# The last work of two routed layers: 32 pairs of tiles and 7 single tiles in place of 39 pairs

## The chip, the cores and the metric

The kernel runs on one core of a Trainium2 chip. A core has five engines with their own instruction streams, which meet only at semaphores: TensorE (PE, matrix products into PSUM), VectorE (DVE), ScalarE (ACT), GpSimd (POOL) and SyncE (SP, which here issues DMAs only). The metric is the device time of one launch in microseconds (us), lower is better. All times below are of one core, and the profile is of one execution.

## The reference, cut to what matters

Input x has 4096 tokens of 128 numbers. The program is a mixture-of-experts layer, an attention-like layer, and the same mixture-of-experts layer again, each added to x:

```python
x = x + 0.5 * ffn(layernorm(x))
x = x + attn(layernorm(x))
x = x + 0.5 * ffn(layernorm(x))

def ffn(h):                                   # D=128, F=512, E=8 experts, K=2 of them per token
    probs = softmax(h @ gate_W.T)
    top_v, top_i = top_k(probs, 2)
    routed = sum over the 2 chosen experts e of
             top_v * ((silu(h @ w1_e[e]) * (h @ w3_e[e])) @ w2_e[e])
    shared = (the same form with 8 small experts, for every token) / 8
    return 0.5 * shared + 0.5 * routed
```

Two choices per token make 8192 (token, expert) rows. They are sorted by expert, and each expert's rows are filled up to whole tiles. All is float32.

## The kernel before, in words

**Two layers.** The loop `for l in range(2)` on every engine does the mixture layer twice; the attention lies between. A layer is: normalise and score the tokens; the shared experts' first chunks ("front", `FRONT` = 7 of 8 chunks of 512 tokens in layer 0, 6 in layer 1) on PE, while DVE and ACT work out the routing; the routed tiles; the remaining shared chunks, while the results come back from DRAM.

**Routing on DVE.** `slots_of` counts each expert's rows, rounds them up, and gives every row a place (`cum`, `pos`). Its steps are a chain: each is followed by a wait for its own semaphore (`route.then`). `batch` turns places into two small one-hot factors that ACT scales (`pairs`) and PE multiplies into `psT`, in 16 batches. `table` makes from it the row numbers (`source`, `target`), and `experts` the weight offset of each pair of tiles (`w_off`). In layer 0 eight `low_part` steps of 128x1024 come after it on DVE.

**Routed tiles.** A tile is 128 rows of one expert; the kernel does `PT` = 2 tiles of one expert as a pair, since both use one set of weights. 8192 rows of 8 experts need at most `PAIRS` = 39 pairs, so `RUN` = 78 tiles a layer, whatever the routing is. POOL fetches a tile's rows with one indirect DMA (`fetch_row`), for groups of `GT` = 4 tiles, three groups ahead; PE transposes them into `psT` (`transpose_rows`); DVE splits the transposed group into a high part `xTH` and a low part `xTL` (`copy_xT`); ACT copies the pair's weights into `w_high` and `w_low` (`weights_of`). Step by step PE then does, by the list of stages and delays of its `pipelined` call, `in_routed` of tile k-4, `look_up` (a register load for the pair's place in W2), `out_routed` of tile k-6, and `transpose_rows` of tile k:

```python
def product(out, a_high, a_low, b_high, b_low):
    pe.matmul(out, a_high, b_high, start=True, stop=False)
    pe.matmul(out, a_high, b_low, start=False, stop=False)
    return pe.matmul(out, a_low, b_high, start=False, stop=True)
```

`in_routed` makes four such products of 256 columns a step, which are half of the hidden features (two of four blocks) of both tiles of the pair: 12 matmuls in the type fp32r. `out_routed` makes 4 plain float32 matmuls of 128x128 a tile. Between them ACT makes `silu` of `psG`, and DVE `hT` = silu times `psU` (`gated_routed`). When a group's last tile is done, DVE scales the four outputs into `yout` (`copy_y`), and POOL scatters them to `results` in DRAM (`send_result`, one indirect DMA a tile, five groups behind the fetch). The last group is shorter (`LAST` = 2 tiles), and its tiles are scaled and sent one by one (`copy_y_last`), from two PSUM banks, `last_y`.

**End of a layer.** SP waits until every tile has been sent (`y_sent`), then loads `results` back: in layer 0 as `Y` in pieces for the attention, in layer 1 as `YF`, which is added into the output. Before that SP's last work in a layer is to write the tokens to DRAM. After its last `out_routed` PE does the remaining shared chunks.

The order of each engine's work is thus fixed by the program text. Lines named in the prediction: 1334 to 1336 (`product`), 1405 (`out_shared`), 1433 (`transpose_rows`), 1487 (`out_routed`), 830 to 854 (`slots_of`), 876 to 879 (`experts`), 908 (`low_part`), 980 (`copy_y`), 626 and 641 (fetch and send).

Of the kernel before, what the change touches and what calls it, by code (L numbers as in the profile page):

```python
# [13 lines left out]
P = 128  # L14
D = 128
NT = 4096
TILES = NT // P
E = 8
# [11 lines left out]
PAIRS = TOPK * NT // PAIR + E - 1  # L30
RUN = PT * PAIRS
TILES_R = RUN
# [130 lines left out]
def macaron(nc, x, w_qkvT, w_swigluT, w_outT, gateT, w1_e, w3_e, w2_e, w1_s, w3_s, w2_s, out):  # L163
    ctx = ExitStack()
    with ctx:
# [14 lines left out]
        def overlaid(*groups):  # L180
# [34 lines left out]
        pair_no = sb("pair_no", [P, PAIRS])  # L215
# [16 lines left out]
        pair_bits = sb("pair_bits", [P, 2, E], i32)  # L232
        npair = sb("npair", [P, E])
        tend = sb("tend", [P, E])
        tstart = sb("tstart", [P, E])
        base = sb("base", [P, E])
        pair_e = sb("pair_e", [P, PAIRS])
        w_off = sb("w_off", [P, PAIRS], i32)
# [24 lines left out]
            [("xTH", [P, 2, GT, P], fp32r), ("xTL", [P, 2, GT, P], fp32r)],  # L263
            [(name, [P, TILES, E], fp32) for name in ("logit", "prob", "cand", "onehot0", "onehot1", "pick")] +
            [(name, [P, E, TILES], fp32) for name in ("chosen", "cum")] +
            [("pair_cmp", [P, PAIRS, E], fp32)])
        xTH = memory["xTH"]
        xTL = memory["xTL"]
        logit = memory["logit"]
# [6 lines left out]
        pair_cmp = memory["pair_cmp"]  # L276
# [12 lines left out]
            [("Y", [P, 4, TOPK, TB, D], fp32), ("XNT", [P, NT], fp32)],  # L289
            [("hs", [P, 2, FT, CH * P], fp32),  # L290
# [7 lines left out]
        XNT = memory["XNT"]  # L298
        hs = memory["hs"]
# [61 lines left out]
        pair_weights = sem("pair_weights")  # L361
        consts = sem("consts")
# [88 lines left out]
        last_y = [psY, psT]  # L451

        block = ctx.enter_context(nc.Block())
        CONSTS = 13
# [6 lines left out]

        first_routed = [l * (SHARED + RUN) + front[l] for l in range(2)]

# [33 lines left out]
        def _(sp):  # L497
# [10 lines left out]
            for l in range(2):  # L508
# [6 lines left out]
                pipelined(sp, [(keep_tokens, 0)], CHUNKS, 2)  # L515

# [31 lines left out]
        def _(pool):  # L548
# [25 lines left out]
            pool.iota(pair_no[:, :], pattern=[[1, PAIRS]], base=0, channel_multiplier=0,  # L574
# [133 lines left out]
        def _(dve):  # L708
# [34 lines left out]
            for l in range(2):  # L743
                def gated(hidden, s, turn):

                    dve.wait_ge(silu_done, turn + 1)
                    dve.wait_ge(u_full, turn + 1)
                    dve.tensor_tensor(hidden, silu[:, s.u % 2, :], psU[:, s.u % 2, :], ALU.mult).then_inc(h_done, 1)  # L748
# [77 lines left out]
                def slots_of():  # L826
# [3 lines left out]
                    route.then(dve.tensor_scalar(pair_bits[:, 0, :], psY[:, E:2 * E], float(PAIR - 1), None, ALU.add))  # L830
                    route.then(dve.tensor_scalar(pair_bits[:, 1, :], pair_bits[:, 0, :], PAIR.bit_length() - 1, None,
                                                 ALU.logical_shift_right))
                    route.then(dve.tensor_copy(npair[:, :], pair_bits[:, 1, :]))
                    route.then(dve.tensor_tensor_scan(tend[:, :], ones[:, 0:E], npair[:, :], 0.0,
                                                      ALU.mult, ALU.add))
                    route.then(dve.tensor_tensor(tstart[:, :], tend[:, :], npair[:, :], ALU.subtract))
                    dve.scalar_tensor_tensor(base[:, :], tstart[:, :], float(PAIR), psY[:, 0:E], ALU.mult, ALU.add)\
                       .then_inc(ranks_read, 1)
# [5 lines left out]
                                                      ALU.mult, ALU.add))  # L844
                    shared_steps(1)
# [27 lines left out]
                def experts():  # L873

                    cmp3 = [P, PAIRS, E]
                    route.then(dve.tensor_tensor(pair_cmp[:, :, :], wide(pair_no[:, :], cmp3),
                                                 tend[:, :].unsqueeze(1).to_broadcast(cmp3), ALU.is_ge))
                    route.then(dve.tensor_reduce(pair_e[:, :], pair_cmp[:, :, :], X_AXIS, ALU.add))
                    dve.tensor_scalar(w_off[:, :], pair_e[:, :], float(E - 1), float(F),
                                      ALU.min, ALU.mult).then_inc(w_off_done, 1)  # L880
# [32 lines left out]
                def copy_xT(s):  # L913
# [14 lines left out]
                    dve.wait_ge(xT_link, g + (GROUPS * l + 1))  # L928
# [19 lines left out]
                def gated_routed(s):  # L948
# [5 lines left out]
                    dve.tensor_tensor(hT[:, s.u // PT % 2, half, :].rearrange("p f c -> p (f c)"), silu[:, s.u % 2, :],  # L954
                                      psU[:, s.u % 2, :], ALU.mult).then_inc(h_done, 1)
# [5 lines left out]
                def copy_y_last(par, t):  # L961
# [4 lines left out]
                    return dve.tensor_scalar(yout[:, par, t, :], last_y[t % 2][:, t * D:(t + 1) * D],  # L966
# [19 lines left out]
                if l == 1:  # L986
# [17 lines left out]
                    def add_sums(n):  # L1004
# [3 lines left out]
                        dve.tensor_tensor(xs, xs, last_y[n % 2][:, :], ALU.add).then_inc(last_added_sums, 1)  # L1008
# [119 lines left out]
        def _(act):  # L1128
            act.wait_ge(consts, CONSTS)
            for l in range(2):  # L1130
# [20 lines left out]
                def silu_of(s, turn):  # L1151
# [3 lines left out]
                    act.activation(silu[:, s.u % 2, :], psG[:, s.u % 2, :], ACT.Silu).then_inc(silu_done, 1)  # L1155

                def silu_shared(k):
                    silu_of(Step.of(k, 2), shared_at(l, k))
# [79 lines left out]
                for k in range(RUN):  # L1238
                    silu_of(Step.of(k, 2), first_routed[l] + k)
# [88 lines left out]
        def _(pe):  # L1328
# [11 lines left out]
            def table_entry(l, s):  # L1340


                key = (l, s.i // PT)
# [320 lines left out]
```

## Time and profile before

| | |
|---|---|
| runs | 731.95 us median of 3 (730.91 to 735.62) |
| profiled execution | span 733.5 us, from the first to the last instruction; the page gives no other time of this execution |
| PE | busy 660.3 us (90%) |
| DVE, ACT, POOL | busy 458.8, 411.3 and 430.6 us (63, 56 and 59%) |
| routed stage of layer 0, layer 1 | 112 to 299 us, 512 to 699 us |
| DMA | 45.91 MB, mean 63 GB/s |

How to read it: an engine's share is over the whole span, though the stages have different limits; so the stretches have to be read one by one. A stage is found in the 40 slices of the page, and its limit in the chain of waits, which is followed back from the last instruction. Matmuls of PE overlap, so the length of one says less than the distance from one start to the next. The plain float32 matmul of 128x128 shows as two records.

### The profile page before, as it was taken

Reading aid. Unit: us, or ns where it says so; the run is one execution under the profiler, and the core shown is the slowest. Engines: PE = TensorE matmul, PEld = TensorE weight load, DVE = VectorE, ACT = ScalarE, POOL = GpSimd, SP = SyncE. Lnnn points to the kernel's source line nnn. Section 1 sums busy time; section 2 is a strip of 40 time slices with the busy share of each in tenths; the row PEclk is TensorE's granted clock in tenths of the full one; section 3 lists DMA queues with packets and bytes.
Section 4 is the critical chain, followed back from the end, with each engine's and each line's share of the span. In section 5 each row is a group of like instructions: output and inputs, shape, how many; then the busy total and the mean of one; then the engine's idle time right before and its main releaser. Section 6 shows DMA issues by size and latency. Waiting matters only on the chain.

```text
span 733.5 us, 14294 instructions
## 1 busy us (share of the span) xinstructions
PE 660.3 (90%) x4860; PEld 602.1 (82%) x4860; DVE 458.8 (63%) x1177; ACT 411.3 (56%) x861; POOL 430.6 (59%) x511
## 2 busy tenths in 40 slices
PE   3878999999999999957987777999999999999995
PEld 3767879999999999825654574888999999999983
DVE  6678895554445555359999867884555555544536
ACT  2658617666666666236654436664666666666520
POOL 5600075777777776489987424007577777777530
PEclk9989999999999999989999997999999999999999
DMA  9542011221222231131100002402212212212137
GB/s 296 231 78 40 1 42 38 56 52 52 52 55 52 52 53 44 57 105 44 47 12 1 0 1 46 73 2 49 40 55 54 52 52 56 51 53 52 43 104 261
DMA packets 35685, 45.91 MB, mean 63 GB/s; under 512 B 6432, under 2 KB 27936, under 8 KB 35232
## 3 DMA queue, kind: packets, MB, share of 16 engines
q1 hardware_dynamic: 25632, 24.39, 11.8%
q0 software_dynamic: 9984, 20.63, 11.5%
q8 instruction: 40, 0.66, 0.4%
q14 instruction: 29, 0.24, 0.1%
HBM read 28.41 MB, written 16.58 MB: 61 GB/s over the span
## 4 chain that ended last, share of the span: by engine, by line
PE 65%; DVE 20%; issue 4%; ACT 4%; POOL 3%; DMA 2%; SPq 1%; ACTq 0%; POOLq 0%; DVEq 0%
PE psY L1487 18%; PE psG L1334 6%; PE psU L1336 6%; PE psG L1336 6%; PE psU L1335 6%; PE psG L1335 6%; PE psU L1334 6%; PE psH L1405 4%; DVE rec L1076 3%; PE psT L1433 2%; DVE hs L748 2%; DVE XN L738 2%; DVE ln_stats L725 1%; DVE xn L1060 1%; POOL results L641 1%
## 5 line engine op out<-in xcount | busy, mean ns | idle before, releaser
L626 POOL DMA_INDIRECT rows<-tokens,source x156 | 153.7, 985 | 156.3 <-DVE source L900 98.6
L1155 ACT ACTIVATE silu<-psG 128x512 f32<-128x512 f32 x220 | 131.1, 596 | 150.6 <-PE psG L1336 147.2
L954 DVE TENSOR_TENSOR hT<-silu,psU 128x512 f32<-128x512 f32 x156 | 107.4, 688 | 158.9 <-PE psU L1336 150.3
L641 POOL DMA_INDIRECT results<-yout,target x156 | 153.8, 986 | 63.3 <-issue 45.7
L1487 PE MATMUL psY<-W,hT 128*128 x1232 | 162.4, 275 | 1.8 <-DVE yout L980 1.8
L1487 PEld LDWEIGHTS psY<-W,hT 128*128 128x128 f32 x1232 | 150.4, 191 | 2.2 <-DVE hT L954 2.2
L1229 ACT ACTIVATE w_high<-W13H 128x1024 fp32r x78 | 82.7, 1061 | 59.0 <-PE psU L1336 54.8
L1334 PE MATMUL psG<-xTH,w_high 128*128 128x256 f32 x312 | 100.0, 321 | 0.7 <-ACT w_low L1229 0.7
L1336 PE MATMUL psG<-xTH,w_low 128*128 128x256 f32 x312 | 88.0, 282 | 0.0
L1336 PE MATMUL psU<-xTH,w_low 128*128 128x256 f32 x312 | 88.0, 282 | 0.0
L1335 PE MATMUL psU<-xTL,w_high 128*128 128x256 f32 x312 | 87.7, 281 | 0.0
L1335 PE MATMUL psG<-xTL,w_high 128*128 128x256 f32 x312 | 87.4, 280 | 0.0
L1334 PE MATMUL psU<-xTH,w_high 128*128 128x256 f32 x312 | 86.9, 278 | 0.0
L1229 ACT ACTIVATE w_low<-W13L 128x1024 fp32r x78 | 81.8, 1048 | 0.0
L748 DVE TENSOR_TENSOR hs<-silu,psU 128x512 f32<-128x512 f32 x64 | 43.7, 684 | 38.3 <-PE psU L1336 30.5
L1405 PEld LDWEIGHTS psH<-W2S,hs 128*128 128x128 f32 x512 | 59.4, 192 | 5.7 <-DVE hs L748 4.7
L1405 PE MATMUL psH<-W2S,hs 128*128 128x128 f32 x512 | 60.1, 276 | 2.9 <-DVE hs L748 2.9
L1334 PEld LDWEIGHTS psG<-xTH,w_high 128*128 128x128 f32 x312 | 59.2, 190 | 0.9 <-issue 0.9
L1335 PEld LDWEIGHTS psG<-xTL,w_high 128*128 128x128 f32 x312 | 59.3, 190 | 0.0
L1334 PEld LDWEIGHTS psU<-xTH,w_high 128*128 128x128 f32 x312 | 59.1, 190 | 0.0
L1336 PEld LDWEIGHTS psG<-xTH,w_low 128*128 128x128 f32 x312 | 58.8, 188 | 0.0
L1335 PEld LDWEIGHTS psU<-xTL,w_high 128*128 128x128 f32 x312 | 58.6, 188 | 0.0
(188 smaller groups left out, 1215.7 us busy)
## 6 DMA issues: line engine op xcount, KB each, us to landing
W<-w_e SPq DMA_DIRECT2D x3, 2048.0 KB, 13.7
tokens<-XN SPq DMA_DIRECT2D x16, 260.0 KB, 5.9
Y<-results SPq DMA_DIRECT2D x32, 128.0 KB, 2.2
YF<-results SPq DMA_DIRECT2D x16, 256.0 KB, 5.9
rows<-tokens,source POOLq DMA_INDIRECT x156
results<-yout,target POOLq DMA_INDIRECT x156, 2.3
X<-x SPq DMA_DIRECT2D x8, 256.0 KB, 5.5
out<-X SPq DMA_DIRECT2D x8, 256.0 KB, 2.8
```

The source lines that it names most:

```text
L626: pool.indirect_dma_start(rows[:, slot(l, g), t, :], None, tokens, bass.IndirectOffsetOnAxis(ap=source[:, tile:tile + 1], axis=0))\
L641: pool.indirect_dma_start(results, bass.IndirectOffsetOnAxis(ap=target[:, tile:tile + 1], axis=0), yout[:, g % 2, t, :], None).then_inc(y_ ...
L748: dve.tensor_tensor(hidden, silu[:, s.u % 2, :], psU[:, s.u % 2, :], ALU.mult).then_inc(h_done, 1)
L954: dve.tensor_tensor(hT[:, s.u // PT % 2, half, :].rearrange("p f c -> p (f c)"), silu[:, s.u % 2, :], psU[:, s.u % 2, :], ALU.mult).then_i ...
L1076: dve.reciprocal(rec[:, s.u, :, :], den[:, s.u, :, :]).then_inc(y_link, 1)
L1155: act.activation(silu[:, s.u % 2, :], psG[:, s.u % 2, :], ACT.Silu).then_inc(silu_done, 1)
L1229: act.activation(used[p % 2][:, :, :], kept[:, :, bass.ds(entries[p], F)], ACT.Copy)\
L1334: pe.matmul(out, a_high, b_high, start=True, stop=False)
L1335: pe.matmul(out, a_high, b_low, start=False, stop=False)
L1336: return pe.matmul(out, a_low, b_high, start=False, stop=True)
L1405: i = pe.matmul(psH[:, par, t * D:(t + 1) * D], hs[:, par, f, t * P:(t + 1) * P], W2S[:, f, :], start=(f == 0), stop=(f == FT - 1))
L1487: i = pe.matmul(into[:, t * D:(t + 1) * D], hT[:, s.u // PT % 2, f, s.u % PT * P:(s.u % PT + 1) * P], W2[:, bass.ds(at + f * D, D)], start ...
```

## The change

The routed work of a layer is now 32 pairs and then 7 single tiles: `RUN` = 71 tiles in 18 groups, of which the last has 3 tiles. Each expert's rows, rounded up to tiles, fill as many pairs as they can, and an odd tile goes to the singles. Six parts follow from it.

1. A single tile has no weights in `w_high` and `w_low`. SP loads the float32 `w1_e` and `w3_e` of its expert from DRAM into one of six homes, `w_single`, two DMAs of 256 KB each, when PE has passed given tiles (single n after tile 6n+7; the seventh, which uses the first home again, after single 0 has been read).
2. PE multiplies them with the float32 `xT_whole`: 8 plain matmuls of 128x128 (`in_single`), all four blocks of one tile, where a pair's step has 12 of 256 columns. DVE makes one copy of the transposed group in place of the high and low part.
3. `out_routed` of a single waits for its own `hT` and looks up its own place in W2.
4. `slots_of` and `experts` have more steps, since places past an expert's pairs are moved to the singles at the end.
5. The last three tiles go to three PSUM banks, and PE's shared chunk that uses the third waits for `y_done`.
6. The tables that are `TILES_R` wide shrink from 78 to 72 columns, and buffers `psG`, `psU` and `silu` go by the running number of the step, since 71 is odd.

```diff
-PAIRS = TOPK * NT // PAIR + E - 1
-RUN = PT * PAIRS
-TILES_R = RUN
+PAIRS = TOPK * NT // PAIR
+PAIRED = PT * PAIRS
+SINGLES = E - 1
+RUN = PAIRED + SINGLES
+TABLES = PAIRS + SINGLES
+TILES_R = RUN + RUN % 2
+SINGLE_HOMES = 6
...
+                sp.wait_ge(w_off_done, l + 1)
+                sp.wait_ge(sh_full, l * CHUNKS + FRONT[l])
+                sp.wait_ge(batch_used, BATCHES_P * (l + 1))
+                for n in range(SINGLES):
+                    if n < SINGLE_HOMES:
+                        sp.wait_ge(u_full, first_routed[l] + 6 * n + 8)
+                    else:
+                        sp.wait_ge(u_full, first_routed[l] + PAIRED + n - SINGLE_HOMES + 1)
+                    entry = sp.value_load(w_off[0:1, PAIRS + n:PAIRS + n + 1], min_val=0, max_val=(E - 1) * F)
+                    home = n % SINGLE_HOMES
+                    for a, w in ((0, w1_e), (1, w3_e)):
+                        sp.dma_start(w_single[:, home, a, :], w[:, bass.ds(entry, F)]).then_inc(single_in[home], 16)
...
+                    route.then(dve.tensor_tensor(past_pairs[:, :], single_end[:, :], lengths[:, 1, :], ALU.subtract))
+                    route.then(dve.tensor_tensor(past_pairs[:, :], past_pairs[:, :], paired_end[:, :], ALU.add))
+                    route.then(dve.tensor_scalar(past_pairs[:, :], past_pairs[:, :], -1.0, float((RUN - 1) * P),
+                                                 ALU.mult, ALU.add))
+                    route.then(dve.scalar_tensor_tensor(chosen[:, :, :], cum[:, :, :], 0.0, wide(past_pairs[:, :], ET),
+                                                        ALU.is_ge, ALU.mult))
+                    route.then(dve.tensor_tensor(cum[:, :, :], cum[:, :, :], chosen[:, :, :], ALU.add))
+                    route.then(dve.tensor_tensor(cum[:, :, :], cum[:, :, :], wide(paired_end[:, :], ET), ALU.add))
...
+                    if g * GT >= PAIRED:
+                        dve.wait_ge(gate_link, g + (GROUPS * l + 1))
+                        dve.tensor_reduce(gate[:, g % RING, 0:n], gate_parts[:, par, 0:n, :], X_AXIS, ALU.add)
+                        dve.tensor_copy(xT_whole[:, par, 0:n, :].rearrange(flat), psT[:, 0:n * P]).then_inc(xT_done, 1)
+                        return
...
+                def in_single(s, par, turn):
+
+                    n, t = s.i - PAIRED, s.u % GT
+                    if t == 0:
+                        pe.wait_ge(xT_done, s.over(GT) + (GROUPS * l + 1))
+                    pe.wait_ge(single_in[n % SINGLE_HOMES], singles_loaded(l, n))
+                    for out, w, used, full in ((psG, 0, silu_done, g_full), (psU, 1, h_done, u_full)):
+                        pe.wait_ge(used, turn - 1)
+                        for f in range(FT):
+                            i = pe.matmul(out[:, turn % 2, f * P:(f + 1) * P],
+                                          w_single[:, n % SINGLE_HOMES, w, f * P:(f + 1) * P],
+                                          xT_whole[:, par, t, :], start=True, stop=True)
+                        i.then_inc(full, 1)
...
                     at = table_entry(l, s)
-                    if s.u % PT == 0:
+                    if s.i >= PAIRED:
+                        pe.wait_ge(h_done, s.i + (first_routed[l] + 1))
+                    elif s.u % PT == 0:
                         pe.wait_ge(h_done, s.i + (first_routed[l] + PT))
...
-                    into = last_y[t % 2] if s.i >= RUN - LAST else psY
+                    into = last_y[l][t] if s.i >= RUN - LAST else psY
```

PE at the end of layer 0's routed work, before (psG, psU: inputs' products; psY, psT: outputs; a group's last whole tile, then the last two):

```order
L1334 MATMUL psU<-xTH,w_high 128x256
L1335 MATMUL psU<-xTL,w_high 128x256
L1336 MATMUL psU<-xTH,w_low 128x256
L1345 TENSOR_LOAD w_off
L1345 ISA x2
L1494 ISA x2
L1487 MATMUL psY<-W,hT 128x128 x4
L1487 MATMUL psY<-W,hT 128x128 [waits y_done,h_done]
L1487 MATMUL psY<-W,hT 128x128 x3
L1487 MATMUL psT<-W,hT 128x128 x4
```

PE at the same place after the change:

```order
L1525 MATMUL psG<-xT_whole,w_single 128x128 [waits silu_done,single_in0]
L1525 MATMUL psG<-xT_whole,w_single 128x128 x3
L1525 MATMUL psU<-xT_whole,w_single 128x128 [waits h_done]
L1525 MATMUL psU<-xT_whole,w_single 128x128 x3
L1405 TENSOR_LOAD w_off
L1405 ISA x2
L1580 ISA x2
L1573 MATMUL psY<-W,hT 128x128 [waits y_done,h_done]
L1573 MATMUL psY<-W,hT 128x128 x3
L1405 TENSOR_LOAD w_off
L1405 ISA x2
L1580 ISA x2
```

The seventh single's input product stands before the outputs of the last group's first tile; before the change the last group's outputs followed one another with no input product between.

DVE in `slots_of` of layer 0, before (from the first count to the shared step after it):

```order
L830 TENSOR_SCALAR pair_bits<-psY 128x8 [waits ranked]
L831 TENSOR_SCALAR pair_bits<-pair_bits 128x8 [waits route_link]
L833 CAST npair<-pair_bits 128x8 [waits route_link]
L834 SCALAR_TENSOR_TENSOR tend<-ones,npair 128x8 [waits route_link]
L836 TENSOR_TENSOR tstart<-tend,npair 128x8 [waits route_link]
L837 SCALAR_TENSOR_TENSOR base<-tstart,psY 128x8 [waits route_link]
L840 SCALAR_TENSOR_TENSOR chosen<-base,chosen 128x8 [waits ranks_read]
L842 SCALAR_TENSOR_TENSOR cum<-not_first,chosen 128x256 [waits route_link]
L748 TENSOR_TENSOR hs<-silu,psU 128x512 [waits u_full,silu_done,route_link]
```

The same place after the change, from `cum` on (ahead of it stand eight steps of 8 or 16 elements in place of seven of 8):

```order
L879 SCALAR_TENSOR_TENSOR cum<-not_first,chosen 128x256 [waits route_link]
L882 TENSOR_TENSOR past_pairs<-single_end,lengths 128x8 [waits route_link]
L883 TENSOR_TENSOR past_pairs<-past_pairs,paired_end 128x8 [waits route_link]
L884 TENSOR_SCALAR past_pairs<-past_pairs 128x8 [waits route_link]
L886 SCALAR_TENSOR_TENSOR chosen<-cum,past_pairs 128x256 [waits route_link]
L888 TENSOR_TENSOR cum<-cum,chosen 128x256 [waits route_link]
L889 TENSOR_TENSOR cum<-cum,paired_end 128x256 [waits route_link]
L784 TENSOR_TENSOR hs<-silu,psU 128x512 [waits u_full,silu_done,route_link]
```

Six steps stand between `cum` and the shared step, each waiting for the one ahead of it.

## Rows read from the trace of the kernel before

**Rows 1.** The page: busy time of engines; granted TensorE clock in 40 slices.

```profile
PE 660.3 (90%) x4860; PEld 602.1 (82%) x4860; DVE 458.8 (63%) x1177; ACT 411.3 (56%) x861; POOL 430.6 (59%) x511
PEclk9989999999999999989999997999999999999999
```

**Rows 2.** Busy time by stretch: routed stages of layer 0 and 1; first line names columns.

```profile
core 0: us, PE busy (x) PEld busy (x) DVE busy (x) ACT busy (x) POOL busy (x), PEclk, DMA share, GB/s
112.00:299.00 187.00, 186.58 (x1618) 186.44 (x1618) 94.59 (x173) 119.74 (x155) 133.89 (x137) 1.00 0.21 50
...
512.00:699.00 187.00, 186.85 (x1623) 186.65 (x1622) 95.08 (x174) 117.72 (x152) 133.59 (x137) 1.00 0.20 50
```

**Rows 3.** Chain of waits, PE in layer 0: start us, length us, what.

```profile
67.98 3.57 PE psH L1405 x32
...
127.26 0.89 PE psY L1487 x8
...
131.88 0.89 PE psY L1487 x8
...
134.62 0.89 PE psY L1487 x8
...
296.89 0.12 PE psG L1334
...
298.31 0.91 PE psY L1487 x8
```

**Rows 4.** Chain of waits, behind the routed stage of layer 0, then layer 1.

```profile
299.24 0.70 DVE yout L980
...
306.59 2.23 DMA results<-yout,target
...
309.28 2.22 DMA Y<-results
...
709.87 5.69 DMA YF<-results
```

**Rows 5.** POOL in order of time, layer 0: start, length, idle before and releaser.

```profile
300.20 0.97 POOL L641 DMA_INDIRECT results<-yout,target  x1 [4.43 <-DVE yout L980]
...
306.59 0.97 POOL L641 DMA_INDIRECT results<-yout,target  x1 [0.30 <-issue]
```

**Rows 6.** Chain of waits, ahead of the routed stages: layer 0, then layer 1.

```profile
44.65 0.44 DVE onehot L796
...
51.92 0.19 DVE chosen L840
...
91.14 0.40 DVE pair_cmp L876
91.57 0.49 DVE pair_e L878
...
455.50 0.19 DVE chosen L840
...
492.45 3.57 PE psH L1405 x32
```

**Rows 7.** PE in order of time, and a stretch as in Rows 2: clock of layer 1.

```profile
444.60 0.50 PE L1334 MATMUL psU<-XNTH,W13SH 128*128 128x512 f32 x1 [0.59 <-DVE hs L748]
...
449.39 0.79 PE L1334 MATMUL psG<-XNTH,W13SH 128*128 128x512 f32 x1 [3.83 <-ACT silu L1155]
...
450.00:454.00 4.00, 3.52 (x11) 2.22 (x9) 3.76 (x12) 0.60 (x1) 0.24 (x1) 0.50 0.00 0
```

**Rows 8.** DMA issues: what, queue, count, KB each, median us to landing.

```profile
W<-w_e SPq DMA_DIRECT2D x3, 2048.0 KB, 13.7
...
W13S<-w_s SPq DMA_DIRECT2D x2, 256.0 KB, 4.3
```

**Rows 9.** The page, costliest groups: shapes, count | busy us, mean ns | idle, releaser.

```profile
L1155 ACT ACTIVATE silu<-psG 128x512 f32<-128x512 f32 x220 | 131.1, 596 | 150.6 <-PE psG L1336 147.2
L954 DVE TENSOR_TENSOR hT<-silu,psU 128x512 f32<-128x512 f32 x156 | 107.4, 688 | 158.9 <-PE psU L1336 150.3
```

More of the change, by code:

```diff
@@ L275, in macaron @@
         cum = memory["cum"]
[L276 removed]
+        tile_cmp = memory["tile_cmp"]
+        single_cmp = memory["single_cmp"]
         memory = overlaid(
@@ L361, in macaron @@
         pair_weights = sem("pair_weights")
+        single_in = [sem(f"single_in{n}") for n in range(SINGLE_HOMES)]
         consts = sem("consts")
@@ L450, in macaron @@
         psQKV = [psG, psH]
-        last_y = [psY, psT]
+        last_y = [[psY[:, :], psT[:, :], psH[:, (FRONT[l] - 1) % 2, :]] for l in range(2)]
         block = ctx.enter_context(nc.Block())
-        CONSTS = 13
+        CONSTS = 15
         SHARED = CHUNKS * FT
@@ L462, in macaron, with singles_loaded @@
         first_routed = [l * (SHARED + RUN) + front[l] for l in range(2)]
+        def singles_loaded(l, n):
+            before_it = sum(1 for m in range(SINGLES) if m % SINGLE_HOMES == n % SINGLE_HOMES)
+            return 32 * (l * before_it + n // SINGLE_HOMES + 1)
         def fetched(l, g):
@@ L747, in gated @@
                     dve.wait_ge(u_full, turn + 1)
-                    dve.tensor_tensor(hidden, silu[:, s.u % 2, :], psU[:, s.u % 2, :], ALU.mult).then_inc(h_done, 1)
+                    dve.tensor_tensor(hidden, silu[:, turn % 2, :], psU[:, turn % 2, :], ALU.mult).then_inc(h_done, 1)
                 def gated_shared(s):
@@ L953, in gated_routed @@
                     half = bass.ds(s.u % PT * (FT // PT), FT // PT)
-                    dve.tensor_tensor(hT[:, s.u // PT % 2, half, :].rearrange("p f c -> p (f c)"), silu[:, s.u % 2, :],
-                                      psU[:, s.u % 2, :], ALU.mult).then_inc(h_done, 1)
+                    dve.tensor_tensor(hT[:, s.u // PT % 2, half, :].rearrange("p f c -> p (f c)"), silu[:, turn % 2, :],
+                                      psU[:, turn % 2, :], ALU.mult).then_inc(h_done, 1)
                 def copy_xT_later(s):
@@ L1154, in silu_of @@
                         act.wait_ge(h_done, turn - 1)
-                    act.activation(silu[:, s.u % 2, :], psG[:, s.u % 2, :], ACT.Silu).then_inc(silu_done, 1)
+                    act.activation(silu[:, turn % 2, :], psG[:, turn % 2, :], ACT.Silu).then_inc(silu_done, 1)
                 def silu_shared(k):
-                    silu_of(Step.of(k, 2), shared_at(l, k))
+                    silu_of(shared_at(l, k))
                 def pairs(b):
@@ L1340, in table_entry @@
             def table_entry(l, s):
-                key = (l, s.i // PT)
-                if key not in entries:
-                    entries[key] = pe.value_load(w_off[0:1, s.i // PT:s.i // PT + 1], min_val=0, max_val=(E - 1) * F)
-                return entries[key]
+                n = s.i // PT if s.i < PAIRED else PAIRS + s.i - PAIRED
+                if (l, n) not in entries:
+                    entries[l, n] = pe.value_load(w_off[0:1, n:n + 1], min_val=0, max_val=(E - 1) * F)
+                return entries[l, n]
             for l in range(2):
@@ L1360, in in_shared @@
                         pe.wait_ge(silu_done, turn - 1)
-                    product(psG[:, s.u % 2, :], W13SH[:, 0, tile], W13SL[:, 0, tile], XNTH[:, chunk], XNTL[:, chunk])\
+                    product(psG[:, turn % 2, :], W13SH[:, 0, tile], W13SL[:, 0, tile], XNTH[:, chunk], XNTL[:, chunk])\
                         .then_inc(g_full, 1)
@@ L1364, in in_shared @@
                         pe.wait_ge(h_done, turn - 1)
-                    product(psU[:, s.u % 2, :], W13SH[:, 1, tile], W13SL[:, 1, tile], XNTH[:, chunk], XNTL[:, chunk])\
+                    product(psU[:, turn % 2, :], W13SH[:, 1, tile], W13SL[:, 1, tile], XNTH[:, chunk], XNTL[:, chunk])\
                         .then_inc(u_full, 1)
```

94 lines of the change are left out of this document (63 added, 31 removed).

## The prediction

> **What bounds the kernel now.** First the page [rows 1]: PE is busy for 90% of the span and no other engine for more than 63%; the granted clock is near full except in two or three slices. So I ask in which stages PE sets the pace. The stretches [rows 2] answer for the two routed stages: in 187 us each PE is busy 186.6 and 186.9 us at clock 1.00 (2.4 GHz), ACT 118 to 120, POOL 134, DVE 95. Together they are 374 of 733.5 us, and in them only PE's work counts. The chain of waits shows what a tile costs PE there [rows 3]. From the first input product (296.89) to the output product (298.31) are 1.42 us: 12 matmuls of 256 columns. The output product takes 0.89 us: 4 plain float32 matmuls of 128x128, 0.223 us each. That makes 2.31 us, and two steps (127.26 to 131.88, start of an output to start of an output) take 4.62, so nothing else stands between. A step with a group's transposes takes 2.74 (131.88 to 134.62), so 0.43 for four tiles, 0.11 for one. The same float32 form in the shared experts gives the same price: 16 matmuls in 3.57 us, 0.223 each [rows 3].
>
> Behind the routed stage the chain leaves PE [rows 4]: from the last whole group's output it goes to DVE's scaling (299.24), to POOL's sends, of which the last lands from 306.59 on, and to the loads of the results (309.28 in layer 0, 709.87 in layer 1). PE's last two tiles and its remaining shared chunk are not on it. Ahead of the routed stage the chain runs through DVE's routing in both layers, and in layer 0 also through the steps that find the pairs' experts (91.14, 91.57); in layer 1 those stand beside PE's own work (492.45) [rows 6].
>
> **The change part by part, for one layer.** I count up to the scaling of the last whole group, since the chain leaves PE there. Before, 78 input products and 76 output products stand ahead of it. After, the last whole group is tiles 64 to 67; ahead of its scaling stand 64 input products of pairs, 6 of singles (two steps of lead) and 68 outputs.
>
> - Input products: 14 of the old kind go, 14 x 1.42 = 19.9 us. Six singles come, each 8 plain matmuls of 128x128: 8 x 0.223 = 1.78, so 10.7 us. Net -9.2.
> - Output products: 8 fewer x 0.89 = -7.1.
> - Transposes: 7 tiles fewer x 0.11 = -0.8.
> - Sends: POOL then sends 4 + 3 tiles where it sent 4 + 2. From 300.20 to 306.59 are five intervals, 1.28 us each [rows 5], so +1.3. POOL has the time to be there: it waited 4.43 us for the scaling before [rows 5], and the last three outputs are there in time: PE needs 1.78 + 3 x 0.89 = 4.45 us for them after the last whole group, whose four sends take 5.1.
>
> That is -15.8 a layer, -31.5 us for both.
>
> The waits that a single adds on PE cost nothing as I see it. Its hidden values are asked for two steps later, behind another input product of 1.78 us. Its register load stands behind that product too; two steps of a pair hold one such load and take 4.62 us, twice the matmuls [rows 3], so 1.42 us cover it there. Behind the last tile only the outputs of the last group are uncovered, and they are not on the chain. ACT copies no weights for singles, and DVE makes one copy of a group in place of two; both were idle for a third or more of the stage [rows 2], so neither gives a gain.
>
> The loads of single weights stand on SP, which had nothing left to do but wait for the sends. The first six are asked for after tiles 7, 13, ... 37 and used at tiles 64 to 69, over 60 us later. The seventh is asked for when PE has read single 0, and used five tiles later, 5 x 2.67 = 13.4 us. Two loads of 256 KB of the shared weights landed in 4.3 us, and those of 2 MB in 13.7 [rows 8]. At either end of that range the wait is 0 to 0.3 us; I take 0, since the first row has the same size.
>
> The routing costs. Six steps come between the places and the next shared step: three of 8 elements at 0.20 us (as 51.92, with its wait) and three of 256 at 0.44 to 0.45 (as 44.65), 1.95 us [rows 6]. The seven small steps ahead become eight, of which two need no wait of their own: about -0.1. So +1.85 us, on the chain in both layers [rows 6]. In `experts` the two steps of 0.40 and 0.49 lose some 0.1 of waiting, and five or six of 7 to 56 elements come at 0.1 to 0.2: +0.9, on the chain in layer 0 only. Together 2 x 1.85 + 0.9 = +4.6 us. Its bounds are 2.3 (half hidden, since DVE also has pauses later) and 9.2 (twice, if shared steps held up by it wait again). Narrower tables (72 columns for 78) give back a few tenths, which I leave in the bounds.
>
> The longer routing makes PE wait longer at a place where its clock is in doubt. The row: after a pause of 3.83 us PE runs at 0.50, which is 1.2 GHz, in the 4 us behind 450, while a pause of 0.59 us changed nothing [rows 7]. The Trainium skill, "TensorE: Matmul & The Clock Gate", section "Why this matters for your kernels", asks for no long pauses between bursts of matmuls, since the clock falls back to half. By that rule another slow stretch would be paid for; by the row, 1.85 us more lies between the two pauses and decides nothing. I take no fall, and keep it as a rival.
>
> Sum: -31.5 + 4.6 = -26.9 us. On the profiled execution, 733.5 of span, this gives 706.6. The median of the runs is 1.55 below that span, so I say **705 us**. Ends: -34.1 (no extra send on the chain) + 2.3 = -31.8 gives 700; -31.5 + 9.2 = -22.3 gives 710.
>
> **The rivals.**
> A second slow-clock stretch in the routing of each layer. For it: PE already falls to 1.2 GHz in this place, and the pause grows. Against: DVE sets the pace there, so slow matmuls are partly hidden. The stretch at 0.50 shown is 4 us long [rows 7]; at half speed it costs half its length, 2 us a layer, and one of twice the length 4 us: 705 + 4 to 8 = 709 to 713.
>
> The singles don't pipeline. If each output product had to stand still for its own silu and `hT`, 0.60 and 0.69 us [rows 9], 14 singles would lose 18 us: 723. Against it: PE's order has two steps between. This would be a change that gives about half of what its counts say.
>
> The single weights come late; this one ends on the other side. Place: the wait of each single's first matmul. Price: if the two loads are asked for only when PE stands there, or the indirect fetches and the loads hold each other up so far, each single waits 4.3 us [rows 8], 14 x 4.3 = 60 us: 765, slower than before. The point from which it decides: a load that lands after PE's arrival, over 60 us for six of seven; to lose the whole gain, the 14 singles have to wait 1.9 us each. Against it: DMA's mean share in the stage is 0.20 to 0.21 [rows 2], and 3.5 MB more a layer in some 170 us is 21 GB/s beside 50. The Trainium skill has a rule that makes this rival dearer (same page, section "Loop structure matters more than you think"): waits for a DMA between matmuls let the clock fall. By it the singles would also run at half speed, 14 x 2.67 = 37 us on top, 802. Nothing in the trace of before shows a matmul that waits for a load in this stage.
>
> **How the numbers follow.** The forecast has 0.77, its own range 700 to 710. The clock rival has 0.14 (709 to 713), singles that don't pipeline 0.04 (half of it within 1%), late weights 0.05. About 1%, 7.3 us, is what a measurement here can tell from no change, since the three runs lie 4.7 us apart. The range of 699 to 712 holds the forecast with its bounds and most of the clock rival. Faster by over 1%: 0.77 + 0.14 + 0.02 = 0.93, set at 0.92 for what I have not seen; within 1% 0.03; slower 0.05.
>
> **What would show it.** Right: a routed stage some 17 us shorter up to the last whole group's scaling in each layer, PE still busy without a pause in it; input products of singles that take 1.78 us from the first matmul to the output product; seven sends at the end instead of six, 1.28 us apart, the first of them after an idle POOL; the routed stage starting some 2.7 us later in layer 0, counted from the start, and 1.8 us later in layer 1, counted from the end of the attention. Wrong: PE idle ahead of the singles' first matmul with a DMA as releaser (late weights); idle ahead of their outputs with `hT` as releaser (no pipelining); more time at 1.2 GHz in the routing (clock); a chain that at the end of the routed stage goes through POOL's earlier sends and not through DVE's scaling, by which PE would no longer be the bound.

## The result and the profile after

| | before | after |
|---|---|---|
| runs | 732.58 us median of 4 (730.91 to 735.62) | 709.18 us median of 4 (706.52 to 710.24) |
| profiled execution, span | 733.5 us | 706.9 us |
| PE busy | 660.3 us | 632.6 us |

The ratio is 0.9654, interval [0.9633, 0.9675]: 3.5% faster. The forecast was 705, range 699 to 712; its sum said -26.9 us on the span of the profiled execution. The two spans differ by 26.6, the two medians of this first comparison by 23.4.

The page after, rows as in [rows 1], and the DMA row of the new loads (what, queue, count, KB each, median us to landing):

```profile
PE 632.6 (89%) x4622; PEld 572.5 (81%) x4622; DVE 440.8 (62%) x1167; ACT 375.0 (53%) x819; POOL 401.6 (57%) x485
...
PEclk9999999999999999979999997799999999999999
...
w_single<-w_e SPq DMA_DIRECT2D x28, 256.0 KB, 3.1
```

PE has 27.7 us less work, and the span lost 26.6. The two routed stages after, as in [rows 2] (stretch, then busy us of PE, PEld, DVE, ACT, POOL, granted clock, DMA share, GB/s):

```profile
113.90:283.70 169.80, 169.76 (x1478) 169.60 (x1479) 83.03 (x154) 101.09 (x132) 118.46 (x122) 1.00 0.26 71
...
500.90:670.80 169.90, 169.90 (x1485) 169.90 (x1484) 83.70 (x154) 99.45 (x130) 118.73 (x122) 1.00 0.26 71
```

PE has no pause in either, as before; the other engines have less to do, and DMA moves 71 GB/s in place of 50. So the stage is shorter because PE's work in it is, and by nothing else. The chain of waits through the singles and the end of both layers (start us, length us, what), to be read beside [rows 3, 4]:

```profile
266.31 0.89 PE psY L1573 x8
267.21 0.89 PE psG L1525 x8
268.10 0.89 PE psU L1525 x8
268.99 0.89 PE psY L1573 x8
...
280.04 0.89 PE psY L1573 x8
280.93 0.89 PE psG L1525 x8
281.83 0.89 PE psU L1525 x8
282.72 0.91 PE psY L1573 x8
...
283.65 0.70 DVE yout L1040
...
284.62 0.97 POOL results L677
...
292.27 2.23 DMA results<-yout,target
...
294.95 3.45 DMA Y<-results
...
670.73 0.70 DVE yout L1040
...
683.30 5.65 DMA YF<-results
```

A single is 0.89 + 0.89 of input products and 0.89 of output, one behind the other, 2.68 us from output to output (280.04 to 282.72), with no wait between: neither the load of its weights nor its `hT` is late. From the last whole group's scaling (283.65; 299.24 before) the chain goes on through POOL, as before. In layer 1 that scaling starts at 670.73, and `YF` at 683.30 where it was 709.87: 26.6 us earlier, all that the program gained.

### The profile page after: what moved, and what is told of

It reads as the page before. It is cut to its first block, busy times and chain, and to the rows that moved or that the text cites. A ratio compares the mean times of both kernels' runs of the same rounds, so it can differ in the third digit from the quotient of the medians.

```text
span 706.9 us, 13752 instructions
## 1 busy us (share of the span) xinstructions
PE 632.6 (89%) x4622; PEld 572.5 (81%) x4622; DVE 440.8 (62%) x1167; ACT 375.0 (53%) x819; POOL 401.6 (57%) x485
## 4 chain that ended last, share of the span: by engine, by line
PE 64%; DVE 20%; issue 4%; POOL 4%; ACT 4%; DMA 3%; SPq 1%; POOLq 0%; ACTq 0%; DVEq 0%
PE psY L1573 17%; PE psU L1394 5%; PE psG L1394 5%; PE psU L1395 5%; PE psU L1396 5%; PE psH L1467 5%; PE psG L1395 5%; PE psG L1396 5%; DVE rec L1136 3%; PE psT L1495 2%; DVE XN L774 2%; DVE hs L784 2%; PE psU L1525 2%; PE psG L1525 2%; DVE ln_stats L761 1%
## 5 line engine op out<-in xcount | busy, mean ns | idle before, releaser
L662 POOL DMA_INDIRECT rows<-tokens,source x142 | 138.9, 978 | 156.6 <-DVE source L955 101.3
L1573 PE MATMUL psY<-W,hT 128*128 x1104 | 145.5, 275 | 0.0
L1573 PEld LDWEIGHTS psY<-W,hT 128*128 128x128 f32 x1104 | 134.6, 191 | 0.2 <-DVE hT L1014 0.2
L1289 ACT ACTIVATE w_high<-W13H 128x1024 fp32r x64 | 67.8, 1060 | 48.1 <-PE psU L1396 43.4
L1394 PE MATMUL psG<-xTH,w_high 128*128 128x256 f32 x256 | 82.4, 322 | 0.7 <-ACT w_low L1289 0.7
L1395 PE MATMUL psG<-xTL,w_high 128*128 128x256 f32 x256 | 71.6, 280 | 0.0
L1396 PE MATMUL psG<-xTH,w_low 128*128 128x256 f32 x256 | 71.6, 280 | 0.0
L1395 PE MATMUL psU<-xTL,w_high 128*128 128x256 f32 x256 | 71.5, 279 | 0.0
L1394 PE MATMUL psU<-xTH,w_high 128*128 128x256 f32 x256 | 71.5, 279 | 0.0
L1396 PE MATMUL psU<-xTH,w_low 128*128 128x256 f32 x256 | 71.5, 279 | 0.0
```

What stands on the lines that cost most here:

```text
L662: pool.indirect_dma_start(rows[:, slot(l, g), t, :], None, tokens, bass.IndirectOffsetOnAxis(ap=source[:, tile:tile + 1], axis=0))\
L1289: act.activation(used[p % 2][:, :, :], kept[:, :, bass.ds(entries[p], F)], ACT.Copy)\
L1573: i = pe.matmul(into[:, t * D:(t + 1) * D], h, W2[:, bass.ds(at + f * D, D)], start=(f == 0), stop=(f == FT - 1))
```

## The experiments

They were timed in two batches, each on one chip and beside the kernel before: e1 to e4 (before 735.15 us) and e5 to e8 (before 735.48 us).

**e1, the changed kernel again,** the yardstick of e2 to e4.

> The changed kernel as it is, beside the others on one chip. Theory (TensorE's counts: fewer and cheaper tiles in a stage that TensorE bounds, less one more send and a longer routing): again some 25 us under the kernel before, ratio 0.963 to 0.968. If the first comparison was favoured by chance: over 0.970.

Measured: 708.28 us median (705.51 to 711.07, five runs), ratio 0.9645 [0.9627, 0.9663]. The gain is 26.9 us, the forecast's sum to a tenth; the tenth is luck, since these five runs lie 5.6 us apart, the first comparison gave 23.4 and e6, the same order of work but for its loads, gives 27.3. The medians of the kernel before moved up by some 3 us from the first comparison.

**e2, each of the last seven tiles sent by itself.** It asks whether POOL's sends are the chain's end, as the term "one more send" says.

```diff
-        last_y = [[psY[:, :], psT[:, :], psH[:, (FRONT[l] - 1) % 2, :]] for l in range(2)]
+        last_y = [[psY[:, :], psT[:, :]] for l in range(2)]
+        single_y = [[psY[:, :], psH[:, (FRONT[l] - 1) % 2, :], psH[:, FRONT[l] % 2, :]] for l in range(2)]
...
-                    if last and t < LAST - 1:
-                        pool.wait_ge(y_part, (LAST - 1) * l + t + 1)
+                    if tile >= PAIRED and t < GT - 1 and tile < RUN - 1:
+                        pool.wait_ge(y_part, (SINGLES - 2) * l + tile - PAIRED + (1 if tile < PAIRED + GT else 0))
...
-                    if s.i >= RUN - LAST:
-                        copy_y_last(s.u // GT, s.u % GT).then_inc(y_done if s.i == RUN - 1 else y_part, 1)
+                    if s.i >= PAIRED:
+                        whole = s.i == RUN - 1 or s.u % GT == GT - 1
+                        copy_y_single(s, s.u // GT, s.u % GT).then_inc(y_done if whole else y_part, 1)
...
-                    if c == FRONT[l] + 1:
+                    if c >= FRONT[l]:
                         pe.wait_ge(y_done, GROUPS * (l + 1))
```

> The seven single tiles are scaled and sent one by one as they are done, in place of a group of four and then three; nothing else moves. Theory (the chain leaves TensorE at the scaling of the last whole group and runs through seven sends of 1.28 us): the last send starts some 5.4 us after the output of tile 67 in place of 8.6, so 3.2 us less in layer 0; in layer 1 some 2 us less, since TensorE's remaining shared chunks then end last. Together 4 to 6 us under the changed kernel, ratio to before near 0.958. Rival (the loads of the results, or TensorE's shared chunk, set the end whatever the sends do): no difference to the changed kernel.

Measured: 706.2 us (705.31 to 707.19), ratio 0.9606 [0.9592, 0.962], 2.1 us below e1. The right direction, half of the size or less. Its POOL does what was meant (start, length, idle before and releaser):

```profile
285.41 0.97 POOL L678 DMA_INDIRECT results<-yout,target  x1 [1.71 <-DVE yout L1027]
288.57 0.97 POOL L678 DMA_INDIRECT results<-yout,target  x1 [2.19 <-DVE yout L1027]
...
291.12 0.97 POOL L678 DMA_INDIRECT results<-yout,target  x1 [0.30 <-issue]
```

But the chain has left POOL:

```profile
288.32 0.89 PE psY L1575 x8
...
295.66 3.85 PE psH L1469 x32
...
299.54 0.69 DVE X L799
...
302.01 1.56 DVE xn L1122 x2
```

The results are there, and the attention's first normalisation now waits for PE's remaining shared chunk and DVE's addition of it (299.54). It starts at 302.01, where it started at 302.41 in the profile after, although this execution's routed stage began 1.1 us later (first fetch 93.71, 92.58 there). In layer 1 the chain's end is PE alone. So the send term was right for the changed kernel, and little is to be had behind it: PE is next. Counted from the start of the routed stage (115.07 here, 113.94 after), the normalisation of layer 0 comes 1.5 us sooner, and from PE's last shared product ahead of the routed stage of layer 1 to the end of the span are 1.8 us less (497.08 to 704.4; 497.77 to 706.9). That is 3.3 us in these two executions, of which the later start of the routed stage took back 1.1.

**e3, the six new routing steps done twice in each layer,** the second time into spare tiles that nobody reads (the same sizes, each in the chain).

```diff
...
                     route.then(dve.tensor_tensor(cum[:, :, :], cum[:, :, :], wide(paired_end[:, :], ET), ALU.add))
+                    route.then(dve.tensor_tensor(spare_e[:, :], single_end[:, :], lengths[:, 1, :], ALU.subtract))
+                    route.then(dve.tensor_tensor(spare_e[:, :], spare_e[:, :], paired_end[:, :], ALU.add))
+                    route.then(dve.tensor_scalar(spare_e[:, :], spare_e[:, :], -1.0, float((RUN - 1) * P),
+                                                 ALU.mult, ALU.add))
+                    route.then(dve.scalar_tensor_tensor(spare_et[:, :, :], cum[:, :, :], 0.0, wide(spare_e[:, :], ET),
+                                                        ALU.is_ge, ALU.mult))
+                    route.then(dve.tensor_tensor(spare_et[:, :, :], cum[:, :, :], spare_et[:, :, :], ALU.add))
+                    route.then(dve.tensor_tensor(spare_et[:, :, :], spare_et[:, :, :], wide(paired_end[:, :], ET), ALU.add))
                     shared_steps(1)
```

> The six added routing steps on VectorE are done a second time, into spare tiles, in both layers. Theory (they stand on the chain ahead of both routed stages at 1.95 us): 3.9 us more than the changed kernel, ratio to before near 0.971. Rival one (half hidden behind VectorE's later pauses): 2 us more or less. Rival two (the longer pause of TensorE brings a longer stretch at 1.2 GHz): 6 us more or above, with a lower granted clock in the routing.

Measured: 714.15 us (713.83 to 714.64), ratio 0.9717 [0.9704, 0.973], 5.9 us above e1. The copies take 1.98 us in each layer (55.08 to 57.06 in layer 0), so 4.0 us are the steps, on the chain in both layers; in layer 1 they are all that is added (from ACT's step of 1.28 us behind the attention to PE's last shared product ahead of the routed stage are 65.02 us, 63.04 in e1). The clock accounts for a part of the other 2 us. Stretches of this kernel (columns as in [rows 2]):

```profile
52.00:58.00 6.00, 2.66 (x11) 1.82 (x11) 5.49 (x18) 2.38 (x4) 0.00 (x0) 0.98 1.25 192
58.00:64.00 6.00, 6.00 (x36) 5.86 (x36) 5.76 (x21) 3.56 (x12) 0.00 (x0) 0.72 0.21 34
448.00:452.00 4.00, 0.78 (x3) 0.64 (x4) 3.69 (x11) 0.60 (x1) 0.00 (x0) 0.93 1.23 190
452.00:456.00 4.00, 4.00 (x24) 3.90 (x23) 3.80 (x14) 0.83 (x4) 0.00 (x0) 0.62 0.93 143
```

PE is busy for 2.66 of 6 us while DVE routes, and in the stretch behind it the clock is 0.72; the same in layer 1 behind 448 to 452. A product of a shared chunk, 3.57 us at full clock, takes 5.20 us there (chain, from 58.77). e1's profile has no such stretch between 52 and 64 us: its clock is 1.00. But the stage starts only 0.85 us later by it: from the shared step behind the routing (57.06) to the first routed product (117.82) are 60.76 us, 59.91 in e1. Nor do the copies alone bring it: e2 and e4, whose routing is that of the changed kernel, have the same stretch and a product of 5.20 and 5.19 us. So rival two is seen only in part, and about 1 us of the 5.9 stays open.

**e4, the singles with the pairs' arithmetic:** ACT makes `w_high` and `w_low` for them too, PE does 24 matmuls of 128 columns in fp32r in place of 8 plain ones, and no weights come from DRAM.

```diff
...
-                            i = pe.matmul(out[:, turn % 2, f * P:(f + 1) * P],
-                                          w_single[:, n % SINGLE_HOMES, w, f * P:(f + 1) * P],
-                                          xT_whole[:, par, t, :], start=True, stop=True)
+                            cols = slice(f * P, (f + 1) * P)
+                            i = product(out[:, turn % 2, cols], w_high[n % 2][:, w, cols], w_low[n % 2][:, w, cols],
+                                        xTH[:, par, t, :], xTL[:, par, t, :])
...
```

> The seven singles keep the arithmetic of the pairs: weights split in memory and copied by ScalarE, 24 matmuls of 128 columns in the type fp32r a tile, no loads from DRAM. It does the half of the change that is fewer tiles, without plain float32. No row shows such a matmul with 128 columns. If it takes half of the 0.118 us of 256 columns: 1.41 us a tile in place of 1.78, and ScalarE (2.1 us of copies and 0.6 us of silu) sets 2.7 us a tile, so the same time as the changed kernel within 2 us. If it takes 0.11 us, as a transpose of 128 columns does: 2.64 us a tile, 12 us more, ratio near 0.982. If few columns make it much slower, 0.235 us: 5.6 us a tile, 54 us more, slower than before.

Measured: 718.99 us (718.14 to 719.79), ratio 0.9778 [0.9764, 0.9791], 10.7 us above e1. Two singles on its chain:

```profile
278.62 0.94 PE psY L1561 x8
...
282.19 0.94 PE psY L1561 x8
```

3.57 us from output to output, where the plain form takes 2.68: +0.89 a single, and six of them a layer stand ahead of the last whole group's scaling: 12 x 0.89 = 10.7, all of the difference. So PE's products in this place are paid for one to one. A matmul of 128 columns costs (3.57 - 0.89) / 24 = 0.112 us (0.110 with the 0.94 shown here for the output), hardly less than one of 256 columns, 1.42 / 12 = 0.118 [rows 3]; this is the second of the three cases foreseen. So in the pairs' form a single tile's input product costs 2.68, nearly the 2.84 of a pair with both tiles, and the plain form's third of the matmuls is what makes it 1.78.

**e5, late loads:** each single's weights are asked for only when PE has done the input product before. The rival "late single weights", made to happen.

```diff
-                    if n < SINGLE_HOMES:
-                        sp.wait_ge(u_full, first_routed[l] + 6 * n + 8)
-                    else:
-                        sp.wait_ge(u_full, first_routed[l] + PAIRED + n - SINGLE_HOMES + 1)
+                    sp.wait_ge(u_full, first_routed[l] + PAIRED + n)
```

> Each single's two weight loads of 256 KB are asked for only when PE has made the input product of the tile before it, in place of over 60 us ahead. Theory (the forecast's rival 'late single weights'): the 14 singles wait for their loads. A load of this size landed 3.1 us after its issue in the changed kernel; the output product that stands between hides 0.89 us and the issue of two loads adds some tenths, so 2.5 to 3.5 us a single, 35 to 49 us in all: 743 to 757 us, and a gain that is lost. If the waits also take PE's clock to 0.5 in this place, the singles' matmuls (2.67 us each at full clock) cost up to 14 x 2.67 = 37 us more: 780 to 794 us. If the loads were late in the changed kernel already, or cost nothing wherever they stand, the time stays at 708.

Measured: 779.53 us (773.75 to 782.4), ratio 1.0571 [1.0531, 1.0611]: the whole gain lost, and 44 us more. Its chain:

```profile
276.46 0.02 issue
...
277.62 3.06 DMA w_single<-w_e
...
280.72 1.45 PE psG L1522 x8
282.17 1.72 PE psU L1522 x8
...
285.03 3.05 DMA w_single<-w_e
...
288.12 1.97 PE psG L1522 x8
290.08 1.72 PE psU L1522 x8
...
296.12 2.08 PE psG L1522 x8
```

A single takes 7.4 to 8.0 us (280.72, 288.12, 296.12) in place of 2.68. From the end of one input product to the start of the next are 4.26 us (276.46 to 280.72), of which the output product would have filled 0.89: 3.37 lost, 14 x 3.37 = 47 us. The rest goes with the clock: the same 8 records take 1.72 us where they took 0.89 (granted clock 0.50 from 282.2 to 283.9, which is 1.2 GHz for 2.4), and PE's input product takes 3.2 to 3.8 us in place of 1.78; 14 times 1.4 to 2.0 is 20 to 28 us. Together 67 to 75; the profiled spans differ by 73.7. The Trainium skill, "TensorE: Matmul & The Clock Gate", section "Loop structure matters more than you think", has this rule, that waits for a DMA between matmuls let the clock fall; this trace agrees, with 1.72 us for 0.89 and a granted clock of 0.50.

**e6, loads in a burst:** all six first singles' loads asked for after the eighth routed tile.

```diff
-                        sp.wait_ge(u_full, first_routed[l] + 6 * n + 8)
+                        sp.wait_ge(u_full, first_routed[l] + 8)
```

> The first six singles' loads (twelve of 256 KB) are all asked for after the same routed tile, the eighth, in place of one single every sixth tile. Theory that DMA has room to spare in the routed stage (share 0.26 in the changed kernel): no change, 708 +- 2 us, PE without a pause. Rival, that the loads and the indirect row fetches hold each other up: 3 MB at once delay the fetches of the next groups, PE waits for rows near the stage's start; a group's fetches are three groups ahead (some 28 us), so a pause needs a burst longer than that: up to 5 us a layer, 713 to 718.

Measured: 708.18 us (707.84 to 710.37), ratio 0.9634 [0.9614, 0.9655]: as e1. Twelve loads of 256 KB were issued from 132.81 on within 9.2 us (SP's queue), the median load landed in 4.1 us in place of 3.1, and PE had one wait in the whole stage, 0.7 us at its start, the same as in the profile after:

```profile
132.81 9.22 SPq L547 DMA_DIRECT2D w_single<-w_e  x12
```

So the spacing of the loads is worth nothing here; being ahead of PE is worth 71 us.

**e7, PE kept busy in two pauses of the routing,** with products that nobody reads: 18 in layer 0 ahead of the ranking, 16 in layer 1 ahead of the fourth shared step.

```diff
...
+                def keep_busy(n):
+                    pe.wait_ge(logits_out, CHUNKS * (l + 1))
+                    for _ in range(n):
+                        pe.matmul(psY[:, P:2 * P], ident[:, :], ident[:, :], start=True, stop=True)
...
+                    if l == 1 and k == RANK_STEP[1]:
+                        keep_busy(16)
...
+                    if l == 0 and k == RANK_STEP[0]:
+                        keep_busy(18)
```

> PE does 18 and 16 plain float32 matmuls of 128x128, whose result nobody reads, in the pause ahead of the ranking of layer 0 (4.62 us in the changed kernel) and in the pause of layer 1 ahead of its fourth shared step (3.83 us): 4.0 and 3.6 us at 0.223 each. Theory (the pauses bring the granted clock to 0.5, and the slow stretch behind them is paid for on the chain): the clock stays at 1.0 from 46 to 50 and from 436 to 449 us; on the chain psU before psH goes from 1.66 to 0.9 us and psH from 4.46 to 3.57 in layer 1, and in layer 0 six matmuls of 512 columns go from 0.43 to 0.23: together -2.5 to -4 us, 704 to 706 us, and a smaller spread of the runs than the 5.6 us of the changed kernel. Rival (DVE sets the pace there, the slow matmuls are hidden): within 1 us of 708. Second rival (the filler delays PE's own work): up to +2.

Measured: 706.19 us (706.07 to 708.01), ratio 0.9612 [0.9595, 0.9628]; 2.0 us below e6 of the same batch. The intervals of the two overlap, so the direction is likely and the size unsure. The stretches of e7:

```profile
46.00:50.00 4.00, 4.00 (x18) 3.23 (x18) 2.96 (x14) 3.21 (x5) 0.00 (x0) 1.00 0.59 165
52.00:58.00 6.00, 4.53 (x23) 4.25 (x24) 5.69 (x18) 2.10 (x4) 0.00 (x0) 0.72 1.19 182
434.00:438.00 4.00, 2.08 (x10) 1.27 (x10) 3.46 (x8) 1.33 (x3) 1.16 (x1) 1.00 0.00 0
438.00:444.00 6.00, 3.78 (x10) 2.20 (x10) 5.55 (x21) 0.68 (x2) 0.00 (x0) 0.72 0.81 176
444.00:448.00 4.00, 4.00 (x33) 3.87 (x34) 3.76 (x12) 0.67 (x2) 0.00 (x0) 1.00 1.23 188
```

Behind the filled pauses (46 to 50, 434 to 438) the clock is now 1.00. It falls later, behind the next pauses, of 2.52 us (before 53.47) in layer 0, of 1.67 and 0.58 us (before 437.70 and 439.32) in layer 1, for a shorter time. So the theory was half right: the pause did bring the clock down, but filling one moves the fall to the next. Of the 2.3 us between the spans of e7's and e6's profiles, the routing of layer 0 gives 1.2 (first routed product at 113.48, 114.66 in e6) and that of layer 1 nothing (62.78 and 62.76 us from ACT's step behind the attention to PE's last shared product). The rest goes with the first load of `Y`, which the filler does not touch: POOL waits 4.02 us for it, 5.32 in e6. How much of the gain is the filler's is thus not shown.

**e8, e7's filler and e2's sends together.**

> The filler matmuls of e7 together with the sends of e2 (the last seven tiles scaled and sent one by one). If the two gains are of different places (the clock in the routing, the end of the routed stage) they add: e2's 706.2 less 2.5 to 4, 702 to 704 us. If e2's chain through PE's remaining shared chunk or the clock makes one eat the other: 705 to 706.

Measured: 705.06 us (703.89 to 707.07), ratio 0.9587 [0.9567, 0.9608]: the lowest of all; not the full sum of 702 to 704, and its interval overlaps those of e2 and e7. Against the changed kernel, 0.9654 [0.9633, 0.9675], and e6 of the same batch, 0.9634 [0.9614, 0.9655], it is a gain. In its profile the slow stretch of layer 1 is back (granted clock 0.53 from 438 to 449), and from ACT's step behind the attention to PE's last shared product are 64.48 us, 1.7 more than in e7.

## Why the prediction was right

**PE bounds the routed stage, and the counts of products give its gain: right.** From the first input product to the scaling were 186.8 us (112.42 to 299.24) and are 169.7 (113.94 to 283.65): -17.1, where the three terms said -17.1 (9.2, 7.1 and 0.8). Layer 1's scaling starts 28.15 us earlier, layer 0's 15.6. The rows of the chain that this section reads, before and then after:

```profile
112.42 0.36 PE psG L1334
...
447.45 1.28 ACT L1155
...
508.71 3.84 PE psH L1405 x32
...
698.88 0.70 DVE yout L980
```

```profile
113.94 0.36 PE psG L1394
...
434.47 1.28 ACT L1215
...
497.77 3.84 PE psH L1467 x32
```

e4 shows the same from the other side: 0.89 us more of products a single lengthen the program by 12 times that.

**One more send, +1.3: right.** From the scaling to the load of `Y` were 10.04 us and are 11.30: +1.26, with POOL idle 5.94 us ahead of the first send. In layer 1, from the scaling to the load of `YF`, it is +1.58 (10.99 and 12.57). e2 shows what the term was good for, and its limit.

**Loads and waits of singles at 0: right.** In the profile they cost nothing; e5 shows that this was the step with the highest stake, e6 that a burst early in the stage costs nothing.

**The routing, +4.6: right in mechanism, smaller in size.** Between `cum` and the shared step stand the six steps as counted:

```profile
52.02 0.17 DVE L882 TENSOR_TENSOR past_pairs<-single_end,lengths 128x8 f32<-128x8 f32 x1
...
52.63 0.42 DVE L886 SCALAR_TENSOR_TENSOR chosen<-cum,past_pairs 128x256 f32<-128x256 f32 x1
53.09 0.42 DVE L888 TENSOR_TENSOR cum<-cum,chosen 128x256 f32<-128x256 f32 x1
53.55 0.42 DVE L889 TENSOR_TENSOR cum<-cum,paired_end 128x256 f32<-128x256 f32 x1
54.01 0.69 DVE L784 TENSOR_TENSOR hs<-silu,psU 128x512 f32<-128x512 f32 x1
```

They take 1.99 us (predicted 1.95), and the steps of `experts` 0.91 more than before (0.9 said). Layer 0's routed stage started 1.52 us later, where 2.75 was said: DVE came to `cum` 0.83 us earlier (51.30, 52.13 before), and the steps between the places and `experts`, many of them on the shorter tables, gave back 0.55. Layer 1 lost 2.04 (1.85 said): ACT's step of 1.28 us behind the attention stood 12.98 us earlier (447.45 to 434.47), PE's last shared product ahead of the routed stage only 10.94 (508.71 to 497.77). Together 3.6 in place of 4.6.

**A term that was missing, +1.2.** The first load of `Y` took 2.22 us [rows 4] and takes 3.45 (3.23 in e1, 3.53 in e6). It made good for the routing's smaller cost, so the sum fell nearer than its terms, by luck. It does not belong to the change alone: POOL waits 5.24 us for it in the profile after, but 4.02 in e7's, as before. Why it takes longer in some executions is open; no run was made for it.

**From span to time, -1.55: wrong in size.** The prediction read 706.6 as a span and took off the distance of the median before from the span of the profiled execution. But those are two different executions. In the runs that have both, the time is 1.7 to 1.9 us above the span of the same execution (708.63 and 706.9 here). So a span of 706.6 stands for a time of 708.3 to 708.5; e1 gave 708.28, e6 708.18, and the first comparison 709.18. The 705 lay low by this step, not by the counts.

**The clock rival (0.14): not in the profile of after, but in some executions.** The prediction took the 4 us of its row [rows 7] for the length of the slow stretch; in the trace before, the clock is at 0.50 for some 10 us there (448 to 459) and for some 7 in layer 0 (45 to 52). The profile after has one such stretch in layer 0 (46 to 50 us, shorter than before) and one of some 13 us in layer 1; layer 1's cost of 2.04 us holds it (in e6 and e7, where the chain runs on DVE in this place, the same distance grew by 1.5):

```profile
434.00:450.00 16.00, 11.47 (x35) 8.29 (x36) 12.66 (x40) 4.67 (x9) 3.26 (x3) 0.57 0.61 104
```

e2 to e5 show a second stretch in layer 0 (56 to 64 us). It stands behind a pause of PE for DVE's routing, 2.35 to 3.34 us long in them; in the profile after, e1 and e6 that pause is 1.18 to 1.88 us and the clock stays at 1.00, and the kernel before has none there. The product behind it loses 1.6 us (5.20 for 3.57), the start of the routed stage some 0.9: from the shared step behind the routing to the first routed product are 60.8 us in e2 to e5, 59.9 in after, e1 and e6. The changed kernel's runs lie 3.7 and 5.6 us apart (e1), those of e2 to e4 less than 2; of its first four runs those with a mean granted clock of 0.966 took 709.7 and 710.2, those with 0.975 and 0.977 took 708.6 and 706.5. The runs of e1 and e6 don't keep to this order (708.5 at 0.980, 710.4 at 0.975), so the clock is not all of the spread. The rival's mechanism is borne out; its price of 2 to 4 us a layer was too high, with 0.9 in layer 0 and 0.5 in layer 1 in these profiles, up to 1.7 in layer 1 of e8.

**The rival "late single weights": its mechanism shown, its condition not met.** With the condition made (e5), 779.5 lies between the 765 by the load alone and the 802 with the clock: the loads landed faster than the 4.3 us taken (3.06), and the singles ran at half speed. **Singles that don't pipeline:** no wait for `hT` on the chain, 2.68 us from output to output; the rival falls.

## What to carry to other kernels

Where one engine is busy for a whole stage, count its instructions up to the point where the chain leaves it, price them from starts to starts, and the stage's gain is known closely, here to a tenth; what stands ahead of the stage and behind it has to be priced by itself, since the chain runs through other engines there. Loads that move off an engine's copies onto a DMA queue are free only as long as they are asked for early: the same loads, late, cost 71 us here, about a third of it with the clock. Once a chain's end is shortened, look first for what stands close behind it, as PE's remaining shared chunk did in e2.

## What the runs showed of the hardware that was not expected

- A matmul of 128x128 by 128 columns in fp32r took 0.110 to 0.112 us, one of 256 columns 0.118: halving the columns saved 5 to 7% (e4).
- Filling a pause of PE kept the granted clock at 1.00 behind it, and the clock then fell behind the next pauses, of 2.52 us in layer 0 and of 1.67 and 0.58 us in layer 1 (e7). In the profile after, a pause of 1.88 us in layer 0 (before 54.75) left it at 1.00, so a pause's length alone does not tell.
- Twelve loads of 256 KB in one burst of 9.2 us beside the indirect fetches cost PE nothing (e6).
